# A routed feed-forward layer in a graph kernel: rows moved by 0/1 matrices on TensorE instead of row tables in DRAM, and weights in 2 MB transfers

## The reference

```python
for d in range(4):                      # depth 4, 16 experts
    logits = xf @ Wr[off:off + cnt].T + br[off:off + cnt]
    sel = take_along_axis(logits, leaf[:, None], axis=1)[:, 0]
    leaf = leaf * 2 + (sel > 0)
def body(acc, params):                  # one expert: 512 -> 2048 -> 512
    w1, bb1, w2, bb2, m = params
    h = gelu(xf @ w1 + bb1)
    y = h @ w2 + bb2
    return (acc + m[:, None] * y, None)
```

## Time and profile before

| | |
|---|---|
| median of three runs | 704.81 us |
| the profiled execution, its own time | 707.41 us |
| span of its trace | 705.6 us |
| PE busy | 553.4 us (78%) |
| PEld, DVE, ACT, POOL busy | 286.6, 189.5, 162.4, 37.9 us |
| chain that ended last | PE 37%, SPq 31%, DMA 12%, issue 6%, ACT 5%, DVE 5% |
| moved by DMA | 159.86 MB, mean 227 GB/s over the span |
| mean granted TensorE clock | 0.916 |

### The profile page before, as it was taken

One profiled execution on the slowest core, in us unless ns is written; L12 is line 12 of the kernel. 1 busy time (PEld: TensorE's weight loads), 2 busy tenths in 40 slices (PEclk: granted clock), 3 DMA queues, 4 the chain that ended last, 5 costly groups with the idle time before them and its releaser, 6 DMA issues.

```text
span 705.6 us, 9916 instructions
## 1 busy us (share of the span) xinstructions
PE 553.4 (78%) x2992; PEld 286.6 (41%) x2992; DVE 189.5 (27%) x573; ACT 162.4 (23%) x549; POOL 37.9 (5%) x37
## 2 busy tenths in 40 slices
PE   1706778889899999998899968768777877797960
PEld 1404445634447465444444433234333433341530
DVE  5745777572520101365111111001100110010101
ACT  1614777502101010030222221112101210121320
POOL 4000000002000000005400000000000000000003
PEclk9957999999999999999999998889888988898995
DMA  9922991000202010003899999999999999999105
GB/s 301 309 60 35 425 420 78 30 0 0 75 0 60 0 59 0 9 0 79 299 406 406 406 405 405 420 408 406 407 369 381 378 374 335 367 372 351 57 24 146
DMA packets 38183, 159.86 MB, mean 227 GB/s; under 512 B 12390, under 2 KB 15546, under 8 KB 20820
## 3 DMA queue, kind: packets, MB, share of 16 engines
q1 hardware_dynamic: 32592, 153.60, 57.2%
q0 software_dynamic: 3360, 3.86, 2.1%
q10 hardware_dynamic: 2212, 2.16, 0.9%
HBM read 145.04 MB, written 14.55 MB: 226 GB/s over the span
## 4 chain that ended last, share of the span: by engine, by line
PE 37%; SPq 31%; DMA 12%; issue 6%; ACT 5%; DVE 5%; POOL 2%; ACTq 1%; DVEq 0%; POOLq 0%
SPq L346 11%; SPq L351 10%; DMA w<-in_L_ffn_W 8%; PE P L769 7%; PE P L863 6%; PE P L779 6%; PE P L906 5%; PE P L788 3%; SPq L289 2%; ACT H L459 2%; ACT H L465 2%; SPq L273 2%; SPq L267 2%; SPq L328 1%; DMA xn<-y_rows,gidx 1%
## 5 line engine op out<-in xcount | busy, mean ns | idle before, releaser
L863 PE MATMUL P<-w,H 128*64 128x512 f32 x512 | 142.2, 706 | 50.7 <-DMA w<-in_L_ffn_W 49.0
L906 PE MATMUL P<-w,FB 128*64 128x256 f32 x1024 | 115.9, 385 | 0.0
L554 ACT ACTIVATE FB<-P,G 128x64 f32<-128x64 f32 x256 | 55.8, 329 | 207.6 <-PE P L880 207.6
L1245 DVE COPY H<-P 128x512 f32<-128x512 f32 x32 | 22.1, 691 | 288.9 <-PE P L863 288.9
L863 PEld LDWEIGHTS P<-w,H 128*64 128x64 f32 x512 | 41.0, 162 | 132.1 <-issue 106.3
L906 PEld LDWEIGHTS P<-w,FB 128*64 128x64 f32 x1024 | 72.8, 138 | 36.7 <-issue 1.8
L623 PE MATMUL P<-H 125*125 125x500 bf16 x176 | 58.6, 408 | 16.1 <-ACT H L465 13.3
L1006 DVE TENSOR_SCALAR H<-iota,small 125x626 bf16<-125x626 f16 x176 | 59.9, 380 | 26.8 <-issue 11.6
L769 PE MATMUL P<-G,XT 128*125 128x512 f32 x120 | 52.0, 592 | 0.0
L779 PE MATMUL P<-C,H 125*128 125x313 f32 (+1 forms) x160 | 42.4, 425 | 0.0
L623 PEld LDWEIGHTS P<-H 125*125 125x125 bf16 x176 | 24.8, 141 | 41.7 <-ACT H L465 27.9
(11 more groups left out here) (253 smaller groups left out, 394.2 us busy)
## 6 DMA issues: line engine op xcount, KB each, us to landing
w<-in_L_ffn_W SPq DMA_DIRECT2D x128, 1024.0 KB, 25.4
x_rows<-xn SPq DMA_DIRECT2D x5, 960.0 KB, 12.5
y_rows<-xn SPq DMA_DIRECT2D x5, 960.0 KB, 21.6
G<-in_L_gnn_W SPq DMA_DIRECT2D x3, 1024.0 KB, 5.3
XT<-x_rows SPq DMA_DIRECT2D x16, 128.0 KB, 26.5
y_rows<-XT ACTq DMA_DIRECT2D x16, 128.0 KB
xs<-in_x SPq DMA_DIRECT2D x1, 1120.0 KB
out<-xs SPq DMA_DIRECT2D x5, 224.0 KB
```

The lines of the kernel that those rows point to most:

```text
L554: g = nc.scalar.activation(hT[:, m, :], P[:, 3 + rd, c * SA:(c + 1) * SA], ACT.Gelu, bias=bT[b][:, m:m + 1])
L863: mm = nc.tensor.matmul(P[g * SA:(g + 1) * SA, h, :], xT[b][:, k, :], w1a[:, k, h, g], start=(k == 0), stop=(k == KD - 1))
L906: mm = nc.tensor.matmul(P[g * SA:(g + 1) * SA, 7, 0:256], hT[:, m, :], w2_sb[b][:, m, g * 256:(g + 1) * 256], start=(m == 0), stop=(m == M ...
```

## The change

Five things change together.

1. **No tables in DRAM.** The zero writes at the start, POOL's scatter, its gathers of `b2` and of the results, and the loads and stores of each tile's rows are gone. SP's first small inputs wait for a clearing of `w3_T` on POOL instead.
2. **`select` (L809 of the new kernel).** Ten matmuls pick the next tile's rows out of the five chunks of `xn`: the stationary operand is a 0/1 matrix `sel` (125 x 64 a chunk, made by DVE by comparing the row's place with the tile's offset), the moving one is `xn` with a step of four values, 256 columns, for each half of the array. [...] DVE copies them out (`copy_rows`, L1271), PE turns them with two 128 x 128 transposes (`turn_rows`, L818), DVE copies these (L1275).
3. **`combine` (L834).** It is applied to the tile before: for each chunk, two matmuls with 64 rows each, one in each half of the array's rows, spread `y_sb` over the 125 rows of the chunk by a 0/1 matrix `slot_of`, and DVE adds the two halves to `xs` (L1316). `slot_of` (128 x 625) is made once a tile by DVE (L1320). Each combine waits for the adds of the one before, since they share PSUM banks 2 and 5. The last tile's combines follow behind the loop, in four pairs of banks in turn. `b2` is added as an extra "tile" whose rows are the 16 vectors of `b2`, before the first one.
4. **Weights.** `W1` and `W2` come in two transfers of 2 MB each, in which a partition holds consecutive rows (two of `W1`, eight of `W2`): packets of 16 KB. With them the row of `W1` on a partition is 4p + k instead of 128k + p, which is why `select` takes every fourth value. Within `first_a` the columns of `W1` are read in the order `(h n g r)`: runs of four values, two runs apart.
5. `y_sb` has one buffer, and the routing tables are kept on all partitions instead of one. DVE has the routing's ids and offsets besides.

The diff, cut to its core (a line of "..." stands for what is left out):

```diff
-            sp.wait_ge(s_zero, 1)
-            blk = ROWS * NCH
-            for rows in (x_dram, y_dram):
-                for at in range(0, ZROWS, blk):
-                    sp.dma_start(rows[at:at + blk, :].rearrange("(p c) n -> p c n", p=ROWS), xn[0:ROWS, :, :]).then_inc(s_yz, 16)
+            sp.wait_ge(s_wz, 1)
...
-                    for k in range(KD):
-                        if k < KD - 1:
-                            sp.wait_ge(s_w1u, (done - 1) * (KD - 1) + k + 1)
+                    for j in range(2):
+                        if j == 0:
+                            sp.wait_ge(s_w1u, (done - 1) * (KD - 1) + 2)
                         else:
                             sp.wait_ge(s_h, done * 2)
-                        sp.dma_start(w1_sb[b][:, k, :], W1[bass.ds(e, 1), k * 128:(k + 1) * 128, :].rearrange("a p n -> (a p) n")).then_inc(s_w1[b], 16)
-                    sp.wait_ge(s_xT, done + 1)
-                    load_rows(1 - b, done + 2)
-                    for q in range(4):
-                        sp.wait_ge(s_l2, 4 * (done - 1) + q + 1)
+                        sp.dma_start(w1_sb[b][:, 2 * j:2 * j + 2, :],
+                                     W1[bass.ds(e, 1), :, :].rearrange("a (p k) n -> p (a k) n", p=128)[:, 2 * j:2 * j + 2, :]).then_inc(s_w1[b], 16)
+                    for h in range(2):
+                        sp.wait_ge(s_l2, 4 * (done - 1) + 2 * h + 2)
+                        sp.dma_start(w2_sb[b][:, 8 * h:8 * h + 8, :],
+                                     W2[bass.ds(e, 1), h * HID // 2:(h + 1) * HID // 2, :].rearrange("a (p m) n -> p (a m) n", p=128)).then_inc(s_w2[b][h], 16)
...
-                act.dma_start(y_dram[bass.ds(at, SA), :].rearrange("s (g n) -> g s n", g=2), y_sb[b][:, 0:256]).then_inc(s_yst[b], 16)
+                nc.scalar.activation(y_sb, P[:, 7, 0:256], ACT.Copy).then_inc(s_ycp, 1)
...
+            def select(i):
+                pe.wait_ge(s_sel, i + 1)
+                for c in range(NCH):
+                    for g in range(2):
+                        mm = nc.tensor.matmul(P[g * SA:(g + 1) * SA, 6, 0:256], sel[0:NC, c, :],
+                                              xn[0:NC, c, :].rearrange("t (p k) -> t k p", k=KD)[:, 2 * g:2 * g + 2, :],
+                                              start=(c == 0), stop=(c == NCH - 1))
+                mm.then_inc(s_xrow, 1)
...
+            def combine(c, banks, more=False):
+                for g in range(2):
+                    mm = nc.tensor.matmul(P[0:NC, banks[g], 0:256], slot_of[g * SA:(g + 1) * SA, c * NC:(c + 1) * NC],
+                                          y_sb[g * SA:(g + 1) * SA, :], start=True, stop=not more, skip_group_check=more)
...
+                mm.then_inc(s_comb, 1)
...
-                w1a = w1_sb[b][:, :, :].rearrange("p k (h g n) -> p k h g n", h=2, g=2)
+                w1a = w1_sb[b][:, :, :].rearrange("p k (h n g r) -> p k h g n r", h=2, g=2, r=4)
...
+                if not more:
+                    combine_last(0)
                 pe.wait_ge(s_hc, 2 * i + 2)
                 turn(4, 1).then_inc(s_hT, 1)
                 if not (end and b):
-                    transpose_rows(1 - b)
+                    select(i + 1)
+                if not more:
+                    combine_last(1)
...
                 second_a(0)
+                if not (end and b):
+                    turn_rows(i + 1)
...
                 for q in range(1, 4):
+                    if not more:
+                        combine_last(q + 1)
                     second_a(q)
...
                 if not (end and b):
-                    copy_inputs(i + 1, 1 - b)
+                    copy_rows(i + 1)
+                for c in range(NCH):
+                    if c == 2 and not (end and b):
+                        copy_inputs(i + 1, 1 - b)
+                        if not (end and b == 0):
+                            selector(sel, SA, i + 2, 0).then_inc(s_sel, 1)
+                    dve.wait_ge(s_comb, 5 * i + c + 1)
+                    for g in range(2):
+                        half = xs[0:NC, c, g * 256:(g + 1) * 256]
+                        add = tt(half, half, P[0:NC, (2, 5)[g], 0:256], ALU.add)
+                    add.then_inc(s_add, 1)
```

More of the change, by code:

```diff
@@ L538, in _ @@
             act.sem_inc(s_ycp, 1)
-            for b in range(2):
-                act.sem_inc(s_yst[b], 16)
             act.wait_ge(s_table, 1)
@@ L893, in tile @@
                         turn(3, 0).then_inc(s_hT, 1)
-                if not (end and b):
-                    pe.wait_ge(s_xr[1 - b], 16 * (p + 1))
+                if not more:
+                    combine_last(0)
                 pe.wait_ge(s_hc, 2 * i + 2)
@@ L938, in _ @@
                 tile(last, b, end=True)
+            pe.wait_ge(s_slot, 2 * last + 3)
+            pe.wait_ge(s_ycp, 2 * last + 3)
+            pe.wait_ge(s_add, 10 * last + 11)
+            for c in range(NCH):
+                if c == 4:
+                    pe.wait_ge(s_fin, 1)
+                combine(c, FREE_BANKS[c % 4])
         @block.vector
@@ L1163, in _ @@
-            eid, pos, row, one, cmpq = (small[0:1, 374 + 28 * i:374 + 28 * (i + 1)] for i in range(5))
+            cmp, val, le = sv(374, NE, MORE), sv(518, NCH, NE), keys
+            eid, pos, row, one, cmpq = (small[:, 374 + 28 * i:374 + 28 * (i + 1)] for i in range(5))
             cmpo = sv(518, TAB + 2 - NE, NE)
-            more, last2, tmp = small[0:1, 744:750], small[0:1, 750:751], small[0:1, 752:756]
-            ts(thr[0:NC, :], iota[0:NC, 0:16], float(SA), None, ALU.mult)
+            more, last2, tmp = small[:, 744:750], small[:, 750:751], small[:, 752:756]
@@ L1181, in _ @@
[L1181 removed]
+            link(nc.vector.tensor_copy(cnt16[:, :], P[:, 6, NCH * NE:(NCH + 1) * NE]))
+            nc.vector.memset(big[:, 0:FIXED], 0.0)
+            link(stt(top[:, FIXED:NE], cnt16[:, FIXED:NE], float(NE), iota[:, FIXED:NE], ALU.mult, ALU.add))
+            link(nc.vector.tensor_reduce(extra[:, 0:1], top[:, FIXED:NE], AX.X, ALU.max))
+            link(ts(big[:, FIXED:NE], top[:, FIXED:NE], extra[:, 0:1], None, ALU.is_equal))
@@ new lines, in _ @@
+            link(ts(cap[:, :], big[:, :], float(SB_), float(SA), ALU.mult, ALU.add))
+            link(tt(top[:, :], cnt16[:, :], cap[:, :], ALU.subtract))
+            link(tt(cmp[:], top[:, :].unsqueeze(2).to_broadcast([128, NE, MORE]),
+                    thr[:, 0:MORE].unsqueeze(1).to_broadcast([128, NE, MORE]), ALU.is_gt))
+            link(nc.vector.tensor_reduce(extra[:, :], cmp[:], AX.X, ALU.add))
+            link(nc.vector.tensor_tensor_scan(cnt16[:, :], ones[:, 0:NE], extra[:, :], 0.0, ALU.mult, ALU.add))
@@ new lines, in _, with selector @@
+            link(ts(row, pos, float(NE), float(SB_), ALU.min, ALU.mult))
+            link(stt(one, pos, float(SA), row, ALU.mult, ALU.add))
+            link(tt(offs[0:NC], keys[0:NC, :].unsqueeze(1).to_broadcast([NC, TAB + 2, NCH]),
+                    one[0:NC, :].unsqueeze(2).to_broadcast([NC, TAB + 2, NCH]), ALU.subtract))
+            def selector(to, n, i, first):
+                off = small[0:NC, bass.ds(518 + i * NCH, NCH)]
+                return tt(to[0:NC], iota[0:NC, first:first + n].unsqueeze(1).to_broadcast([NC, NCH, n]),
+                          off.unsqueeze(2).to_broadcast([NC, NCH, n]), ALU.is_equal)
```

284 lines of the change are left out of this document (150 added, 134 removed).

## The result

The changed kernel takes 738.68 us (median of five runs, 738.59 to 744.52), the kernel before 704.16 us (five runs, 701.31 to 706.07): a ratio of 1.049, 95% interval 1.0447 to 1.0533. It is slower, where 701 us and a range up to 730 were forecast.

A forecast was written before the change was run, and what follows sets the result against it. PE was taken to set the pace of the changed kernel's tiles, at 22.8 us against the queue's 20.5. Terms -19.3 + 1.7 + 27.7 - 14.2 = -4.1 us on the median 704.81 gave 701; range 678 to 730.

The forecast's parts named there:

- start, until the experts' one-hots are cast: Prologue: without zero writes the small loads land by 23 us and block 1 starts near 39.6 instead of 59.42: 19.3 gained.
- routing, from there to tile 0: Ahead of tile 0, DVE's added clearing, ids, offsets and row copy and PE's two transposes delay its start by 1.7 us.
- tiles 0 to 13: Fourteen tiles at 22.8 us, plus 1.9 cold start and 2.2 for extra rows: 323.3 us instead of 309.1, +14.2.
- tile 14: The tile with 32 extra rows: 33.0 us instead of 27.2, +5.8, with its clock full.
- the end: After the last copy: 8.8 us instead of 23.0, SP's ten output issues setting the pace, 14.2 gained.
- `select`, 10 matmuls of 256 columns: In each middle tile on PE: 2.2 us, priced from the second layer's matmuls; 0 to +0.7 for the step, taken as 0.
- rival C: `select` reads one value of four at half speed: +2.2 us on 15 picks, +33, 734 us; chance 0.08.
- The wait before the second combine: In each middle tile PE waits for DVE's adds, which stand behind `copy_rows`: +1.3 us, between 1.0 and 1.6.
- The combine's price: Each visible combine in a tile: 0.43 us of stream, halves running together, plus 0.20 going in and 0.10 back: 0.73.
- a clock below 1 between tiles: Sign that the prediction is wrong as a whole: the granted clock falls below 1 between tiles.
- Rival D: The weights' lag is not the store's and stays at 23.8 us a tile: same time, 701, only waits differ; no chance given.
- 16 KB and 2 MB: Weight packets and transfer size: costed at zero, since PE sets the pace and nothing they save can show.

The follow-up runs named there:

- a_contig: The changed kernel with W1 laid out as before (8 KB packets), so that select reads 256 neighbouring values of xn: 701.39 us.
- a_order: The changed kernel with DVE's two adds of the first chunk ahead of copy_rows, except in the tile with 32 extra rows: 722.77 us.
- a_zeros: The changed kernel with ten zero writes of 960 KB put back ahead of the small loads, and DVE's wait for them: 760.17 us.
- a_onehalf: The changed kernel with both matmuls of a combine on the same first 64 rows of the array: 770.29 us, one run.
- b_store2: The kernel before, with each tile's store to y_rows issued as two DMAs of 64 rows x 1 KB: 671.98 us.
- b_all: b_w16 with the zeros taken from a weight buffer and written behind the small loads and ahead of the weights; row tables kept: 653.38 us.
- b_w16: b_store2 with the changed kernel's 2 MB weight transfers, its reading of W1 and b1, and rows turned with a step of four: 671.26 us.

## Why the prediction was wrong

The sum of the prediction against the profiled executions of the changed kernel and of a_contig, both less that of the kernel before, in us:

| step | forecast | measured | in a_contig |
|---|---|---|---|
| start, until the experts' one-hots are cast (317.65 before) | -19.3 | -20.8 | -22.7 |
| routing, from there to tile 0 (12.3 before) | +1.7 | +4.9 | +0.9 |
| tiles 0 to 13 (309.1 before) | +14.2 | +49.2 (672.27 - 314.00 = 358.3) | +15.3 |
| tile 14 (27.2 before) | +5.8 | +9.5 (36.7) | +5.5 |
| tile 15 until the last copy (16.4 before) | +7.7 | +8.4 (24.7) | +8.4 |
| the end (23.0 before) | -14.2 | -14.0 (9.0) | -13.9 |
| together | -4.1 | +37.1 | -6.5 |

**The term that failed.** "`select`, 10 matmuls of 256 columns ... so 10 cost 2.2" and, in the bounds, "from 0 to +0.7 by that ratio; I take 0". They cost 4.71 us, and with neighbours 2.38. The 15 selections behind the first at 2.33 us too much are 35.0 us, the extra rows' (L948) takes 2.47 us instead of 1.30, and the first costs 1.0 (below): 37.2 together. a_contig took back 37.3 us of median time. The mechanism stood in the text as rival C, at 734 us and a chance of 0.08. The range ended at 730 because C was left out of it; even the +0.7 that the prediction allowed for `select`, 10.5 us on 15 picks, is not in it.

Of the 35.0 us by which tiles 0 to 13 exceed the forecast, 32.6 are this term. The rest of a tile is 0.23 us over (3.2 in all), picking the extra rows takes 3.1 us instead of 2.2, and the cold start of tile 0 (1.9) did not come: its first ten matmuls take 4.51 us.

**Why it was priced so low.** The evidence against C compared two spans of four weight loads (0.55 against 0.42 us) and took their ratio as the cost of the step. These differ in shape, and a group's span tells little of one load: singly, the strided loads of L831 have a median of 216 ns and those of L880 140, a ratio of 1.54, in the same trace. And they were weights, not a moving operand. The nearest row was not near enough, and a bound of +0.7 us from it was no bound. The Trainium skill, SBUF — State Buffer, section "Door 1: The DMA port swizzle", wants two hits in a line of 16 bytes. The runs agree with it at three steps: 2.38 us for neighbours, 2.48 for a step of two (two hits), 4.71 for a step of four (one hit). Runs of four values in the first layer lose nothing either: L861, which reads them, shows 4.46 us for 20, and the kernel before, which reads neighbours, 4.51.

**What held.** The wait before the second combine (1.3 forecast, 1.19 measured, and for the reason given: a_order). The combine's price: 0.73 forecast; 0.63 measured to the next group, and the quarter of the second layer behind it then takes 1.88 us instead of a quarter of 7.06, which is 0.11 more. Its 0.10 for going back to 64 columns is the right size, but the reason given, weights that load in half the time, is not in the rows: 137 ns for the loads of L908 with 64 columns, 140 for those of L880 with 128. The first combine is hidden under the wait for DVE (0.16 us left of 0.79). Two transposes 0.4 (0.37). No waits for weights, and a full clock in the middle tiles. The end: 9.0 us against 8.8. A tile without the mispriced term: 25.36 - 2.33 = 23.0 against 22.8. That a_contig meets the 701 us to half a microsecond is in part luck: by the table its start alone gains 3.4 us more than forecast.

**Routing** was 3.2 us short, and 3.0 of it is the clock, not `select`. The filling matmuls (L551) ahead of the first `select` took 6.66 us in this profiled execution, at a mean granted clock of 0.55 from 300.5 to 307.2 us, that is for the most part 1.2 GHz, where the same eight take 3.70 us at full clock in a_contig; the selector had been ready since 303.2. At full clock, with the step of four, the stage takes 14.2 us in a_zeros and in a_onehalf (295.04 to 309.25 us), 1.9 more than before where 1.7 were forecast. With neighbours it takes 13.2 in a_contig, so the first `select` costs 1.0 us here and not 2.3: DVE's tables become what tile 0 waits for. PE of the changed kernel, then of a_contig:

```profile
300.57 6.66 PE L551 MATMUL P<-xn,ident 125*128 125x512 f32 x8
307.16 4.71 PE L809 MATMUL P<-xn,XT 125*64 125x256 f32 x20
```

```profile
298.81 3.70 PE L551 MATMUL P<-xn,ident 125*128 125x512 f32 x8
302.44 2.38 PE L809 MATMUL P<-xn,XT 125*64 125x256 f32 x20
```

**The clock** fell in two more stretches of the changed kernel's profiled execution, where it stayed full in a_contig's: L691 takes 7.22 us instead of 5.53 (granted clock 0.77 from 135 to 142.3 us), and in tile 14, behind three waits of 0.85, 0.85 and 0.93 us for DVE's adds, L908 and L916 take 7.27 us instead of 5.65 (0.76 from 701.8 to 709 us). With L551 these are 6.2 us, about what this execution was slower than the median (5.8). The prediction had named a clock below 1 between tiles as a sign against it; it fell in one tile of sixteen, and explains 1.6 of the 3.7 us that tile 14 took over its forecast, the step of `select` 2.3.

**Rival D and the cause of the lag.** The prediction took the two-engine store as the cause only "as far as its 23.8 us against 20.5 tell". b_store2 shows it: 20.95 us a tile; and of the 16 landings of a transfer in the kernel before, two are late. So 34 us were to be had for two lines. What the row tables still cost then lies outside the late tiles: the wait for `x_rows` in tile 0 (5.33 us in b_store2), the end (23.0 us against 9.0), and the zero writes, which b_all only moves.

**16 KB and 2 MB** were costed at nothing. In the changed kernel PE sets the pace, and a_contig, with W1 in 8 KB packets, waits for no weights; where the queue sets it, b_w16 shows about 0.1 us a tile, and no difference in the time that can be told.

**Left open:** why the clock fell in these stretches here and not in a_contig, a_zeros or a_onehalf (L551 at full clock in all three); and whether it is the zero writes that hold the three engines in b_all, since no run tests it.

## What to carry to other kernels

Before a layout is changed so that packets grow, look at who reads the result: a step of four in fp32 doubled PE's time for that operand, moving or stationary, and cost 37 us in a change whose total was otherwise forecast within a microsecond (its parts within 3.4). A cost seen in one operand, one shape and one group's span is not a bound for another; a term on which 37 us hang wants the rule's own consequence inside the range. And before data is kept out of DRAM because its transfers disturb others, look at their shape: here the outermost dimension of a small store was the whole lag of the late tiles.

## What the runs showed of the hardware that was not expected

- fp32, 256 moving columns in pairs side by side: 0.119 us an instruction for neighbours, 0.124 for every second value, 0.236 for every fourth (2.38, 2.48 and 4.71 us for 20).
- Stationary operand of 128 columns with a step of four: 40 matmuls with their loads 9.36 us instead of 4.68.
- A store of 128 KB a tile with an outermost dimension of 2 cost the other queue's 8.4 MB a tile some 2.9 us of 23.8.
- With that store, 14 of the 16 landings of a 1 MB transfer lay within 1.6 us and two came 22.4 and 22.5 us behind the first (at 620 us); the lag grew by 5.4 to 5.7 us every two tiles from 358 to 483 us.
- Loads of stationary operands (median ns): 137 with 64 columns in L908 of the changed kernel, 140 with 128 columns in L880 of the kernel before.
